# Four attention layers on one core: maxima from three leading products, and where the stacked keys lie

## The chip, the core and the metric

One core of one Trainium2 chip runs the whole program. The metric is the device time of one execution in microseconds (us). An instruction of TensorE is said to be on PE, of VectorE on DVE, of ScalarE on ACT, of GpSimd on POOL; SP is SyncE, which only issues DMAs and waits. A number like L1826 is a line of the kernel before.

## The reference

2,048 tokens of width 256 go through four layers. Each is cross attention to 1,601 context rows of width 192, with a residual, then a feed-forward part with experts, with a residual. Cut to what matters:

```python
q = (layernorm(x) @ Wq + bq) / sqrt(dh)      # 16 heads of 16 in layers 0, 1, 3; 8 heads of 32 in layer 2
k, v = ctx @ Wk + bk, ctx @ Wv + bv          # 1601 keys
x = x + softmax(q @ k.T) @ v @ Wo + bo       # per head, 2048 x 1601 scores
x = x + experts(layernorm(x))                # differs from layer to layer
```

All is float32.

## The kernel before

**Split products.** A score in float32 is built from bf16 parts. Query and key are each split into three bf16 parts (0 is the leading one), and six of the nine products of parts are kept. For a head of 16, the six lie on top of one another in the contraction of one matmul: `KS` (k_stack) holds key parts 0, 1, 2, 0, 1, 0 on partitions 0 to 95, `QS` (q_stack) holds query parts 0, 0, 0, 1, 1, 2. Partition 96 is the mask or zero, 97 to 99 are ones, against which `QS` carries the negative row maximum in three bf16 parts. In layer 2 (heads of 32) the six take two matmuls (`sub` 0 and 1), the first with the leading three.

**The attention loop.** Tokens are taken 512 at a time (`it`, four of them), heads in four groups `g` (four heads a group, two in layer 2), keys in 13 blocks `k` of 128. I call one `k` a slot: 16 groups of 13, so 208 slots in a layer. In a slot PE computes the scores (`scores`, L1863, 128 keys by 512 queries, bf16, four matmuls in every layer), ACT takes the exponential (L986), and PE multiplies the probabilities of the slot before with the values (`weigh`, L1877, float32). Each `weigh` matmul is 32 columns of stationary wide (64 in layer 2) and writes a 32- or 64-partition part of one PSUM bank, so four (two) of them lie side by side in the array.

**Side jobs.** The row maximum must be known before the scores of its group. It is found one to two groups ahead: a `max` job (L1826) computes 128 queries by 400 or 401 keys into one of three PSUM banks in turn, and DVE reduces it (L1257). A group needs 64 such jobs (32 in layer 2), dealt out as five a slot (two or three in layer 2), besides a few jobs that turn, scale and project (`turn`, `den`, `spread`, `out`, and in the first iteration `turn_x` and `query`). A job waits until DVE is done with the job three before it. The first 88 (44) max jobs of a layer run ahead of the loop (`side_prologue`); I call that the prologue. In the loop two jobs go ahead of the first score matmul and the others are spread behind each of the four score pieces.

**Loads.** All loads of keys, queries and feed-forward weights are issued by SP in program order, on one hardware queue. `next_keys` runs at the start of the feed-forward part of layers 0 to 2: it stores the eight pieces of split keys as POOL finishes them, and in layers 0 and 2, after the fourth and the eighth, waits for them to land and issues 12 loads into `KS` (L461). `load_queries` issues six loads and one of ones (L474 to L480), `store_max_rows` one load of the maxima (L494).

Of the kernel before, what the change touches and what calls it, by code (L numbers as in the profile page):

```python
# [6 lines left out]
P = 128  # L7
NT = T // P
Q = 512
# [26 lines left out]

class Count:
# [27 lines left out]

def side_schedule(g, hpg, first, last):
# [11 lines left out]
    late = [("max", (g + 1) % NG, u, c) for u in range(half, units) for c in range(4)] if nxt1 else []  # L78
    early = [("max", (g + 2) % NG, u, c) for u in range(half) for c in range(4)] if nxt2 else []
# [19 lines left out]
def max_jobs(g, hpg, lo, hi):  # L99
    return [("max", g, u, c) for u in range(lo, hi) for c in range(4)]  # L100
# [35 lines left out]
def build(nc, A, out):  # L136
# [13 lines left out]
    with ctx:  # L150
# [46 lines left out]
        with att:  # L197
# [5 lines left out]
            KS = sb("k_stack", [100, 16, S], bf16, att)  # L203
            V = sb("v", [P, NK, 512], f32, att)
            QS = [sb(f"q_stack{i}", [100, 4, Q], bf16, att) for i in range(4)]
# [9 lines left out]
        with ln2:  # L215
            sb("skip_sums", [P, 4 * 2 * Q + 2 * Q + 16 + Q + NG * Q], f32, ln2)
            sb("skip_keys", [100, 16, S], bf16, ln2)
            sb("skip_values", [P, NK, 512], f32, ln2)
            XN = sb("xn", [P, NT, D], f32, ln2)
# [100 lines left out]
        s_ks = [sem(f"s_ks{g}") for g in range(NG)]  # L320
        s_ql = [sem(f"s_ql{i}") for i in range(4)]
# [59 lines left out]


        @block.sync
        def _(sp):
# [34 lines left out]
            def load_constant_rows(L):  # L419

                ones_flat = const_rows[0:1, 0:S]
                rows = [(96, mask_row if L == 3 else zero_row)]
                if L in (0, 2):
                    rows += [(97, ones_flat), (98, ones_flat), (99, ones_flat)]
                for row, src in rows:
                    sp.dma_start(KS[row:row + 1, :, :], src.unsqueeze(1).to_broadcast([1, 16, S]))\
                      .then_inc(s_ksc, 16)
# [26 lines left out]
            def load_keys(L, g):  # L454

                dh, nsub, hpg = ATT[L]["dh"], ATT[L]["nsub"], ATT[L]["hpg"]
                for row in range(6):
                    part = [0, 1, 2, 0, 1, 0][row]
                    src = k_parts[part].rearrange("(h d) s -> d h s", d=dh)[:, g * hpg:(g + 1) * hpg, :]
                    r, sub = (row, 0) if nsub == 1 else (row % 3, row // 3)  # L460
                    sp.dma_start(KS[r * dh:(r + 1) * dh, 4 * g + sub:4 * g + 4:nsub, :], src)\  # L461
                      .then_inc(s_ks[g], 16)

            def load_queries(L, t, buf):
# [5 lines left out]
                dst = QS[buf]  # L470
                if a["nsub"] == 1:
                    for row, part in enumerate([0, 0, 0, 1, 1, 2]):
                        src = q_parts[part].rearrange("(h d) t -> d h t", d=dh)[:, g * hpg:(g + 1) * hpg, cols]
                        sp.dma_start(dst[row * dh:(row + 1) * dh, :, :], src).then_inc(s_ql[buf], 16)  # L474
                else:
                    for row, part in enumerate([0, 0, 0, 1, 1, 2]):
                        src = q_parts[part].rearrange("(h d) t -> d h t", d=dh)[:, g * hpg:(g + 1) * hpg, cols]
                        r = row % 3
                        sp.dma_start(dst[r * dh:(r + 1) * dh, row // 3::2, :], src).then_inc(s_ql[buf], 16)
                sp.dma_start(dst[96:97, :, :], ones_row).then_inc(s_ql[buf], 16)  # L480

            def store_max_rows(L, g):
# [11 lines left out]
                sp.dma_start(QS[g][96:100, 0:4:a["nsub"], :], src).then_inc(s_mr, 16)  # L494
# [25 lines left out]
            load_keys(0, 0)  # L520
            load_keys(0, 1)

            for L in range(4):
# [8 lines left out]
                if L == 0:  # L532
# [3 lines left out]
                    load_keys(0, 2)  # L536
                    load_keys(0, 3)
# [1727 lines left out]
```

## Time and profile before

| | |
|---|---|
| Time, median of 3 runs | 4478.63 us (4469.84 to 4485.76) |
| Profiled execution: its own time, its span | 4481.04 us, 4479.3 us |
| Granted clock of PE, mean over the span | 0.926 |
| PE busy | 4004.6 us (89%) |
| DVE busy | 2650.2 us (59%) |
| ACT busy | 1937.9 us (43%) |
| POOL busy | 322.4 us (7%) |

The granted clock is a share of 2.4 GHz. A busy PE is one with a matmul in flight; successive matmuls overlap, so the distance between two starts is what one costs, not its duration.

### The profile page before, as it was taken

The numbers are of one execution on the slowest core, as the hardware profiler recorded it, in microseconds if no ns is written. First come the engines' busy times: TensorE is split into PE (matmuls) and PEld (weight loads), VectorE is DVE, ScalarE is ACT, GpSimd is POOL, SyncE is SP. The second block draws the span as 40 slices with busy tenths as digits, with TensorE's granted clock in tenths as the row PEclk, the third lists the DMA queues.
The fourth block names the chain that finished last, engine by engine and source line by source line (L and its number), as shares of the span: only waits on it lengthen the run. The fifth ranks groups of instructions, "written<-read, shape, count | busy, mean of one in ns | idle before, by whom it ended". The sixth has DMA issues, their size and how long they took to land. (4 is left out here: it accounts for less than half of the span.)

```text
span 4479.3 us, 60914 instructions
## 1 busy us (share of the span) xinstructions
PE 4004.6 (89%) x19174; PEld 1813.1 (40%) x19175; DVE 2650.2 (59%) x5801; ACT 1937.9 (43%) x2306; POOL 322.4 (7%) x588
## 2 busy tenths in 40 slices
PE   5999999799899999948993999998889999996894
PEld 2333333566333333335662343443532333333563
DVE  5888785445788888532224555443258887874122
ACT  1567667222166766712331334333103666763110
POOL 2100000200010000040002100000101000000202
PEclk8999999799699999958996999999697999997997
DMA  6000000400000000052104000000400000001145
GB/s 126 25 16 13 13 9 2 82 19 19 24 26 16 10 13 9 1 198 95 32 29 104 26 15 12 12 8 19 66 20 27 20 11 13 10 4 67 61 143 106
DMA packets 131861, 170.58 MB, mean 38 GB/s; under 512 B 30840, under 2 KB 111936, under 8 KB 129539
## 3 DMA queue, kind: packets, MB, share of 16 engines
q1 hardware_dynamic: 121986, 136.07, 11.7%
q0 software_dynamic: 9600, 31.04, 2.4%
q8 instruction: 149, 2.44, 0.2%
q14 instruction: 126, 1.02, 0.1%
HBM read 114.12 MB, written 54.66 MB: 38 GB/s over the span
## 5 line engine op out<-in xcount | busy, mean ns | idle before, releaser
L1257 DVE TENSOR_REDUCE mx<-ps 128x1 f32<-128x400 f32 (+1 forms) x3584 | 1809.0, 565 | 491.1 <-PE ps L1826 482.5
L986 ACT ACTIVATE probs<-ps,zero_col 128x1024 f32<-128x1024 f32 (+1 forms) x1040 | 1113.3, 1111 | 889.5 <-PE ps L1863 889.4
L1826 PE MATMUL ps<-k_stack,q_stack 97*128 97x400 bf16 (+3 forms) x4096 | 1219.5, 347 | 74.5 <-issue 34.8
L1863 PE MATMUL ps<-q_stack,k_stack 100*128 100x512 bf16 (+2 forms) x3328 | 1081.6, 382 | 4.0 <-ACT probs L986 4.0
L1877 PE MATMUL ps<-probs,v 128*32 128x512 f32 (+2 forms) x5824 | 891.9, 607 | 0.2 <-ACT probs L986 0.2
L1826 PEld LDWEIGHTS ps<-k_stack,q_stack 97*128 97x128 bf16 (+1 forms) x4096 | 343.9, 98 | 1173.7 <-DVE mx L1257 712.3
L986 ACT ACTIVATE probs<-ps,mask_col 128x1024 f32<-128x1024 f32 (+1 forms) x416 | 441.0, 1110 | 259.6 <-PE ps L1863 259.6
L1863 PEld LDWEIGHTS ps<-q_stack,k_stack 100*128 100x128 bf16 (+2 forms) x3328 | 324.7, 100 | 315.7 <-ACT probs L986 55.8
L1532 DVE SCALAR_TENSOR_TENSOR x_res<-ps,comb,x_res 128x256 f32<-128x256 f32 x336 | 148.3, 482 | 175.7 <-PE ps L2027 168.6
L1877 PEld LDWEIGHTS ps<-probs,v 128*32 128x32 f32 (+2 forms) x5824 | 140.0, 111 | 228.4 <-issue 220.2
L2027 PE MATMUL ps<-w_down_s,h_t_s 128*128 128x256 f32 x640 | 149.5, 381 | 4.3 <-ACT h_t_s L1088 4.1
L2091 PE MATMUL ps<-w_all,xn_t 128*128 x624 | 144.6, 385 | 3.8 <-ACT xn_t L1056 2.4
L2012 PE MATMUL ps<-xn_t,w_up_s 128*128 128x512 f32 x320 | 147.2, 592 | 0.8 <-issue 0.8
L2070 PE MATMUL ps<-w_all,xn_t 128*128 x312 | 142.7, 600 | 0.4 <-issue 0.4
L2027 PEld LDWEIGHTS ps<-w_down_s,h_t_s 128*128 128x128 f32 x640 | 120.6, 190 | 50.7 <-issue 35.5
L1848 PE MATMUL ps<-wo,o_t 128*128 128x256 f32 x512 | 130.7, 405 | 11.0 <-DVE mx L1257 7.6
L2091 PEld LDWEIGHTS ps<-w_all,xn_t 128*128 128x128 f32 x624 | 118.1, 192 | 43.0 <-issue 28.4
L1056 ACT ACTIVATE xn_t<-ps,tile_bias 128x128 f32<-128x128 f32 x312 | 84.7, 383 | 99.6 <-PE ps L2082 99.4
L1088 ACT ACTIVATE h_t_s<-ps 128x512 f32<-128x512 f32 x80 | 46.7, 596 | 177.0 <-PE ps L2012 176.9
L740 POOL MEMSET wv<- 1x256 f32 x4 | 1.2, 304 | 1670.6 <-DVEq L376 1670.3
L1848 PEld LDWEIGHTS ps<-wo,o_t 128*128 128x128 f32 x512 | 99.3, 200 | 40.7 <-DVE mx L1257 20.5
L2045 PE MATMUL ps<-w_up_s,xn_t 128*128 128x512 f32 x256 | 112.2, 601 | 0.8 <-DVE x_res L1499 0.8
(250 smaller groups left out, 2823.9 us busy)
## 6 DMA issues: line engine op xcount, KB each, us to landing
q_stack<-q_parts SPq DMA_DIRECT2D x384, 64.0 KB, 2.2
k_stack<-k_parts SPq DMA_DIRECT2D x96, 200.1 KB
q_parts<-qk_part SPq DMA_DIRECT2D x32, 384.0 KB, 2.5
w_up<-in_up SPq DMA_DIRECT2D x17, 704.0 KB, 4.3
x_place<-zeros POOLq DMA_DIRECT2D x2, 5120.0 KB, 28.6
k_parts<-qk_part SPq DMA_DIRECT2D x24, 384.0 KB, 3.2
w_all<-in_up SPq DMA_DIRECT2D x5, 1024.0 KB, 21.4
w_all<-in_down SPq DMA_DIRECT2D x5, 1024.0 KB, 23.6
```

Source lines behind the costliest of these rows:

```text
L986: act.activation(PR[pair[0] % 4][0:r, :, :], PS[0:r, 2 * b:2 * b + 2, :], ACT.Exp, bias=mask_col[0:r, k:k + 1] if L == 3 else zero_col[0:r ...
L1257: ins = dve.reduce_max(MX4[g % 2][:, u, c:c + 1], PS[:, bank, 0:CK[c]], AX.X)
L1532: dve.scalar_tensor_tensor(X[:, t, :], PS[:, b, 0:D], c, X[:, t, :], ALU.mult, ALU.add).then_inc(s_yf, 1)
L1826: last = mm(PS[:, bank, 0:CK[c]], QS[g][0:rows, s, qt * P:(qt + 1) * P], KS[0:rows, ks0, CKO[c]:CKO[c] + CK[c]], start=sub == 0, stop=sub ...
L1848: last = mm(PS[:, bank, 0:D], OT[:, g, i * P:(i + 1) * P], WO[:, g, :], start=g == 0, stop=g == NG - 1)
L1863: last = mm(PS[0:r, b + i, :], KS[0:rows, (g * hpg + jj) * nsub + sub, k * P:k * P + r], QS[g][0:rows, slot_of(jj) + sub, :], start=sub == ...
L1877: last = mm(PS[pw * jj:pw * jj + pw, 4, :], V[0:r, k, (g * hpg + jj) * pw:(g * hpg + jj) * pw + pw], PR[used[0] % 4][0:r, i, :], start=k = ...
L2012: last = mm(PS[0:rows, b, :], up[:, k, off + at:off + at + rows], xnT[:, k, c * Q:(c + 1) * Q], start=k == 0, stop=k == 1)
L2027: last = mm(PS[:, b, 0:D], HTF[(c - 1) % 2][0:rows, t, i * P:(i + 1) * P], WDF[par][0:rows, t, :], start=t == 0, stop=t == len(ft) - 1)
L2045: last = mm(PS[:, t % 8, :], xnT[:, k, t * P:(t + 1) * P], WUS[par][:, k * 512:(k + 1) * 512], start=k == 0, stop=k == 1)
L2070: last = mm(PS[:, half, :], XT1[par][:, k * P:(k + 1) * P], w1.rearrange("p a f -> p (a f)"), start=k == 0, stop=k == 1)
L2091: last = mm(PS[:, 4 + par, 0:D], HB[:, q * P:(q + 1) * P], w2.rearrange("p a f -> p (a f)"), start=q == 0, stop=q == NF // P - 1)
```

## The change

1. **Layout, layers 0, 1, 3.** Even heads of a group keep partitions 0 to 99, in another order: the three leading products (key 0 by query 0, key 1 by query 0, key 0 by query 1) on 0 to 47, the mask and the ones on 48 to 51, the other three on 52 to 99. Odd heads have the leading three on 64 to 111, mask and ones on 112 to 115, and four more products on 0 to 63.
2. **Max jobs.** In layers 0, 1, 3 a max job contracts over 49 partitions (0 to 48 or 64 to 112) in place of 97. In layer 2 it is one matmul (the first `sub`, 97 partitions) in place of two. In layers 0, 1, 3 jobs of an even and an odd head alternate.
3. **Order in a slot.** Two jobs (one in layer 2) ahead of the scores, up to two behind the last score, the rest between.
4. **Loads.** A group's keys take 13 loads in place of 6 in layers 0, 1, 3, its queries 15 in place of 7, its maxima 2 in place of 1, its constant rows 8 in place of 4 (layer 3: 8 in place of 1; layer 1: none, in place of 1). The keys of layers 1 and 3 are loaded by POOL, after the eighth split and once all pieces have landed; SP goes on without them.

```diff
+ROWS = ([(0, 0, 0), (16, 1, 0), (32, 0, 1), (52, 2, 0), (68, 1, 1), (84, 0, 2)],
+        [(64, 0, 0), (80, 1, 0), (96, 0, 1), (0, 2, 0), (16, 1, 1), (32, 0, 2), (48, 2, 1)])
+MROW, MAX_ROWS, ALL_ROWS = (48, 112), ((0, 49), (64, 113)), (100, 116)
...
+def max_order(hpg):
+    if hpg == 2:
+        return [(u, c) for u in range(2 * TPQ) for c in range(4)]
+    return [((2 * j + odd) * TPQ + t, c) for j in range(2) for t in range(TPQ) for c in range(4) for odd in range(2)]
...
+def places(n, npair):
+    if npair == 1:
+        return [min(n, 1), max(n - 1, 0) // 2, max(n - 1, 0) - max(n - 1, 0) // 2]
+    ahead, end = min(n, 2), min(max(n - 2, 0), 2)
+    rest = n - ahead - end
+    mid = (rest + 2) // 3
+    return [ahead, (rest - mid + 1) // 2, mid, (rest - mid) // 2, end]
...
                     for u in range(8):
                         store_key_parts(u)
-                        if L != 1 and u % 4 == 3:
-                            wait_landed(kd)
-                            load_keys(L + 1, u // 2 - 1)
-                            load_keys(L + 1, u // 2)
...
+                if L in (0, 2):
+                    for c in staged.landed["key"]:
+                        pool.wait_ge(c.sem, c.at())
+                    for g in range(NG):
+                        load_keys(pool, L + 1, g)
...
-                        for sub in range(nsub):
-                            rows = 97 if sub == 0 else 96
-                            s = slot_of(j) + sub
-                            ks0 = (g * hpg + j) * nsub + sub
-                            last = mm(PS[:, bank, 0:CK[c]], QS[g][0:rows, s, qt * P:(qt + 1) * P],
-                                      KS[0:rows, ks0, CKO[c]:CKO[c] + CK[c]], start=sub == 0, stop=sub == nsub - 1)
+                        lo, hi = MAX_ROWS[j % 2] if nsub == 1 else (0, 97)
+                        last = mm(PS[:, bank, 0:CK[c]], QS[g][lo:hi, slot_of(j), qt * P:(qt + 1) * P],
+                                  KS[lo:hi, (g * hpg + j) * nsub, CKO[c]:CKO[c] + CK[c]], start=True, stop=True)
...
-                            for job in slot[:2]:
-                                side(job)
-                            cut = [2 + n for n in chunk_of(max(len(slot) - 2, 0), 2 * npair)]
+                            jobs = list(slot)
+                            share = places(len(slot), npair)
                             for j in range(npair):
                                 for i in range(2):
+                                    for _ in range(share[2 * j + i]):
+                                        side(jobs.pop(0))
                                     scores(g, k, j, i)
-                                    for job in slot[cut[2 * j + i]:cut[2 * j + i + 1]]:
-                                        side(job)
+                            for job in jobs:
+                                side(job)
```

## Rows read from the trace of the kernel before

**Rows 1.** The page: the costliest DVE group; stores of key pieces, with KB and us to landing.
```profile
L1257 DVE TENSOR_REDUCE mx<-ps 128x1 f32<-128x400 f32 (+1 forms) x3584 | 1809.0, 565 | 491.1 <-PE ps L1826 482.5
...
k_parts<-qk_part SPq DMA_DIRECT2D x24, 384.0 KB, 3.2
```
**Rows 2.** Windows: stretch, length, PE, PEld, DVE, ACT, POOL busy, clock, DMA share, GB/s.
```profile
336.00:448.00 112.00, 111.72 (x674) 39.07 (x666) 97.78 (x207) 82.38 (x82) 0.00 (x0) 1.00 0.05 13
...
2688.00:2800.00 112.00, 110.99 (x528) 42.34 (x526) 56.83 (x117) 44.84 (x43) 0.00 (x0) 1.00 0.04 12
```
**Rows 3.** Timeline of layer 0, an ordinary slot: start, length, engine, line, shape, count, idle before.
```profile
412.68 0.33 PE L1826 MATMUL ps<-k_stack,q_stack 97*128 97x401 bf16 x1
...
412.85 0.38 PE L1863 MATMUL ps<-q_stack,k_stack 100*128 100x512 bf16 x1
...
413.07 0.33 PE L1826 MATMUL ps<-k_stack,q_stack 97*128 97x400 bf16 x1
...
413.46 0.33 PE L1826 MATMUL ps<-k_stack,q_stack 97*128 97x400 bf16 x1
...
413.72 1.07 PE L1877 MATMUL ps<-probs,v 128*32 128x512 f32 x8
...
414.72 0.51 PE L1826 MATMUL ps<-k_stack,q_stack 97*128 97x400 bf16 x2
...
415.10 2.50 DVE L1257 TENSOR_REDUCE mx<-ps 128x1 f32<-128x400 f32 x5 [0.33 <-PE ps L1826]
...
416.55 1.06 PE L1877 MATMUL ps<-probs,v 128*32 128x512 f32 x8
```
**Rows 4.** Timeline of PE in layer 2, a slot with three max jobs.
```profile
2680.05 1.08 PE L1877 MATMUL ps<-probs,v 128*64 128x512 f32 x4
...
2681.06 0.86 PE L1826 MATMUL ps<-k_stack,q_stack 97*128 97x400 bf16 x4
...
2683.07 1.08 PE L1877 MATMUL ps<-probs,v 128*64 128x512 f32 x4
```
**Rows 5.** Layer 3, feed-forward: weight loads of the turning matmuls, then a PE row.
```profile
4231.22 0.14 PEld L2153 LDWEIGHTS ps<-ident,x_expert 128*128 128x128 f32 x1
4231.53 0.40 PEld L2153 LDWEIGHTS ps<-ident,x_expert 64*128 64x128 f32 x3 [0.17 <-issue]
4232.10 0.14 PEld L2153 LDWEIGHTS ps<-ident,x_expert 64*128 64x128 f32 x1 [0.17 <-issue]
...
4236.73 6.73 PE L2172 MATMUL ps<-x_expert_t,w_up 128*128 128x320 f32 x24
```
**Rows 6.** Timelines of SP, POOL, ACT, PE and DVE at the start of layer 0's feed-forward part.
```profile
835.86 7.03 SPq L461 DMA_DIRECT2D k_stack<-k_parts  x12
842.94 22.41 SPq L437 DMA_DIRECT2D k_parts<-qk_part  x4
...
838.16 1.15 POOL L749 TENSOR_TENSOR qk_part<-qk,qk_part 128x512 bf16<-128x512 f32 x1
...
859.78 0.60 ACT L922 ACTIVATE qk<-ps 128x512 f32<-128x512 f32 x1 [22.23 <-DMA k_parts<-qk_part]
...
861.20 1.22 PE L1736 MATMUL ps<-wv,ctx_a 128*128 128x256 f32 x2 [20.96 <-ACT v L933]
...
848.04 0.42 DVE L1431 TENSOR_TENSOR comb<-prob_s,r_s 128x256 f32<-128x256 f32 x1
```
**Rows 7.** Timeline of PE, the same place in layer 2.
```profile
3197.57 1.22 PE L1736 MATMUL ps<-wv,ctx_a 128*128 128x256 f32 x2 [14.65 <-ACT v L933]
```
**Rows 8.** Timeline of SP and PE before the first max job of layer 1.
```profile
1172.42 2.69 SPq L474 DMA_DIRECT2D q_stack<-q_parts  x6
1175.16 0.53 SPq L480 DMA_DIRECT2D q_stack<-const_rows  x1
...
1177.29 8.03 PE L1826 MATMUL ps<-k_stack,q_stack 97*128 97x401 bf16 x17 [8.33 <-issue]
```
**Rows 9.** Timeline of POOL, a load that it issues in layer 1.
```profile
2027.62 0.58 POOL L854 DMA_DIRECT2D w_all<-in_down  x1
```

More of the change, by code:

```diff
@@ L77, in side_schedule @@
     half = units * 3 // 8
-    late = [("max", (g + 1) % NG, u, c) for u in range(half, units) for c in range(4)] if nxt1 else []
-    early = [("max", (g + 2) % NG, u, c) for u in range(half) for c in range(4)] if nxt2 else []
+    late = max_jobs((g + 1) % NG, hpg, half, units) if nxt1 else []
+    early = max_jobs((g + 2) % NG, hpg, 0, half) if nxt2 else []
     jobs = late + early[:6] + ([("turn", (g + 1) % NG)] if nxt1 else []) + early[6:]
@@ L320, in build @@
         s_ks = [sem(f"s_ks{g}") for g in range(NG)]
+        s_kt = [sem(f"s_kt{g}") for g in range(NG)]
         s_ql = [sem(f"s_ql{i}") for i in range(4)]
@@ L380, in key_rows, with load_keys @@
             return P if k < NK - 1 else KREM
+        def load_keys(eng, L, g):
+            dh, nsub, hpg = ATT[L]["dh"], ATT[L]["nsub"], ATT[L]["hpg"]
+            done = s_kt[g] if L in (1, 3) else s_ks[g]
+            heads = k_parts.rearrange("r (h d) s -> r d h s", d=dh)[:, :, g * hpg:(g + 1) * hpg, :]
+            if nsub == 1:
+                for odd in range(2):
+                    for row, part, _ in ROWS[odd]:
+                        eng.dma_start(KS[row:row + dh, 4 * g + odd:4 * g + 4:2, :], heads[part][:, odd::2, :])\
+                           .then_inc(done, 16)
+            else:
+                for i, (_, part, _) in enumerate(ROWS[0]):
+                    sub, r = i // 3, i % 3 * dh
+                    eng.dma_start(KS[r:r + dh, 4 * g + sub:4 * g + 4:2, :], heads[part]).then_inc(done, 16)
         @block.sync
@@ L421, in load_constant_rows @@
                 ones_flat = const_rows[0:1, 0:S]
[L422 to L427, printed above, removed]
+                rows = [mask_row if L == 3 else zero_row] + [ones_flat] * 3
+                for i, src in enumerate(rows):
+                    if ATT[L]["nsub"] == 1:
+                        for odd in range(2):
+                            sp.dma_start(KS[MROW[odd] + i:MROW[odd] + i + 1, odd::2, :],
+                                         src.unsqueeze(1).to_broadcast([1, 8, S])).then_inc(s_ksc, 16)
+                    else:
+                        sp.dma_start(KS[96 + i:97 + i, 0::2, :], src.unsqueeze(1).to_broadcast([1, 8, S]))\
+                          .then_inc(s_ksc, 16)
             def store_key_parts(u):
```

83 lines of the change are left out of this document (44 added, 39 removed).

## The prediction

> **What bounds the kernel now.** I read the page first: DVE's largest group, the reductions of the maxima, spends its idle time almost wholly (482.5 of 491.1 us) waiting for PE's max matmul [rows 1]. So DVE waits for PE, not the reverse. The windows say the same of whole stretches of the loop: in 112 us PE is busy 111.7 and DVE 97.8 in layer 0, and 111.0 against 56.8 in layer 2, both with the clock at 1.00, 2.4 GHz [rows 2]. Then the timeline of one slot, where the costs are distances between starts. In layer 0 a max matmul is followed by the next start after 0.17 us (412.68 to 412.85), a score matmul after 0.22 (412.85 to 413.07), a weigh block with what follows it takes 1.00 (413.72 to 414.72), and a slot repeats every 2.83 us (413.72 to 416.55) [rows 3]. Check: 5 x 0.17 + 4 x 0.22 + 1.00 = 2.73, and 0.10 more lies ahead of weigh. DVE does five reductions in 2.50 us and idles 0.33: it could carry a slot of about 2.5 and no less. In layer 2 a slot of three jobs (six max matmuls) takes 3.02 us, with DVE half idle [rows 2, 4].
>
> **What a change of array shape costs.** Score and max matmuls use all 128 rows and columns of the array; weigh uses strips of 32 columns. The last max of the slot starts at 413.46, streams 0.17, and weigh starts not at 413.63 but at 413.72: 0.09 to 0.10 us lost. Weigh is two rounds of 512 float32 columns; at the 0.87 ns a column that float32 costs (6.73 us for 24 matmuls of 320) that is 0.89, so 0.10 of its 1.00 is lost on leaving [rows 3, 5]. The same loss appears where only the number of rows changes. In layer 3's turning, two matmuls of 128 rows and columns (2 x 0.107 us at this rate, less its rounding) stand before one of 64 rows, but its weight load starts 0.31 us after the first's: 0.10 lost. From there to the next 64-row one is 0.57, of which 0.27 is streaming: 0.30 for two more changes and the loads that they expose. And each 64-row load stands behind 0.17 us of idle loader, marked as issue: it was not drawn ahead [rows 5]. I take 0.096 for the change itself and 0.013 for the bf16 load that can no longer be hidden (the two max matmuls after a weigh take 0.51 to the end of the second, 0.01 more than 0.17 + 0.33), together 0.109 us. A contraction of 49 rows at partition 0 or 64 is such a 64-row shape, so every run of max jobs in layers 0, 1, 3 is now fenced by two changes.
>
> **Layers 0, 1, 3, the loop.** I counted with the schedule's own functions, all 208 slots of a layer. The loop holds 936 max jobs. Before, PE changes shape 415 times (in and out of weigh). After, an ordinary slot reads: 2 max, 2 scores, 1 max, 2 scores, 2 max, weigh, so six changes in place of two; over the layer 1,313, that is 898 more. 898 x 0.109 = 97.9 us more. Against it, 320 runs hold two max jobs, one on each row half. They write different banks, and I expect them to run side by side as the strips of weigh do, which start within a few ns (eight in 1.07 us, where one after the other would need eight times 0.43) [rows 3]. With 0.007 between the two starts a pair saves 0.165: 320 x 0.165 = 52.8 us less. Halving the rows by itself saves nothing, since 97 or 100 rows, 400 or 512 columns, all cost what their columns do at 2.4 GHz, 0.17 and 0.22 [rows 3]. Net +45 a layer, +135 in all. Part of it falls in slots where DVE holds PE up today (the one after `turn`, those with a normalized chunk, those with `out`), and there added PE time is free. I take 8 us of the 98 a layer, an estimate with nothing and 25 as its ends, so +110. Bounds: pair starts 0.007 to 0.172 apart (the latter is no overlap, +158), change 0 to 0.15 us (the second is half of 0.30).
>
> DVE does not become the bound in an ordinary slot: 2.93 us leave it 0.4 idle. The three banks hold: of the last two jobs before weigh, DVE ends the second about 0.1 us after weigh, when the next pair's banks have been free for 0.5. ACT has 2 x 1.06 in a slot.
>
> The Trainium skill, TensorE: Matmul & The Clock Gate, Part 3 (packing small matmuls), says tiles on different row groups run at once, about 4 ns apart, and measured 3.07 times for four such tiles. No row here shows row halves; by the 3.07 each further tile would cost a tenth of a matmul, and my sum would be some 10 us higher.
>
> **Layer 2.** One max matmul in place of two: 468 jobs in the loop x 0.172 (0.167 of streaming and 0.005 to the next start) = 80.5 us less. 97 rows is no 64-row shape, so no change of shape is added. DVE (1.5 us of 3.02) and ACT (1.06) leave room for a slot of 2.50 [rows 2, 4]. The max rows are asked for later in the slot (`turn` now stands at its end), but they need some 5.5 us of the 6 left in the group; no stall. -80.
>
> **Feed-forward, layers 0 and 2.** SP issues 12 key loads (7.03 us) and then the store of the fifth key piece; that store waits behind 2.4 MB, ACT resumes at 859.78 after 22.23 us idle, PE at 861.20 after 20.96 [rows 6]. POOL had the piece ready at 839.3 [rows 6], and a store lands in 3.2 us [rows 1]; so ACT would resume at 842.5, 17.3 us sooner. What is late next: DVE's routing ends at 848.5 [rows 6], while PE would have the rest of its values from 844 to about 851, so nothing takes it back. In layer 2 it is 14.65 us of PE's idle time [rows 7]. With 2 us, an estimate, for a clock that the shorter pause leaves up, -34 in all. The moved loads: 52 on POOL; at 0.58 us each [rows 9] 30 us, at most 2 each, so done well before layer 1 (its first max job comes 316 us after the stall ends) and within layer 2's feed-forward part. Expert weights are asked for one expert ahead and have many us to land beside them.
>
> **Starts of layers 0, 1, 3.** The first max job waits for the loads of queries: seven issues in 3.3 us, 0.47 each; it starts 0.05 after the last of them is through [rows 8]. Eight more issues are 3.7 us, three times 11, and layer 0's queries stand behind 8% more key bytes, 2 us: +13. In the loop SP has 15 issues (7 us) in 37; hidden. Layer 2's prologue now keeps PE less busy and I expect the low clock to reach a few us into its loop, and two issues of maxima in place of one: +4.
>
> **Sum.** 110 - 80 - 34 + 13 + 4 = +13. The profiled execution took 4481.0; the median of the runs is 2.4 lower. 4478.6 + 13 + 2 (rounding toward the profiled one) = 4494.
>
> **Rivals.** (a) *The change of height is cheap, and it ends faster.* Only six turning matmuls a tile show a change of rows, in float32; bf16 streams may need less. Each 10 ns less on 2,694 changes is 27 us, so it decides from 0.10 downward: at 0.05 the time is about 4335, at nothing 4230. For it: bf16 weight loads are short. Against: column strips after bf16 max matmuls cost the same 0.10 [rows 3]. 27%. (b) *The pairs don't overlap, or only partly, or the half loads are exposed.* The float32 loads above cost 0.05 each where 0.30 was lost to two changes; if a half-height bf16 load costs that in place of 0.013, 1,848 runs add 0.04, +74: 4568; no overlap at all +158: 4652. The 0.172 apart can also come from the second waiting for its bank, but the banks are free. 20%. (c) *The moved loads collide*: the store stays late or weights come late, the 34 are not earned: 4528. 5%. (d) *The clock falls in the loop* because a slot has 0.66 us of pauses; were a tenth of the three loops granted the lower level (1.2 GHz), where PE's work takes twice as long, it would be some +200: 4690. Nothing in the windows shows such a fall while PE works [rows 2]. 3%. (e) DVE's stalls absorb more than 8 us a layer, or the layer 2 slots gain from the order: 4450, 5%.
>
> **Chances and range.** My forecast holds 40%, with its own range 4465 to 4530, from 0.09 to 0.12 for a change and 0.007 to 0.03 for a pair. What this measurement can tell from no change is 0.3%, 13.4 us, so 4465 to 4492 is no change: of the 40%, 8 are faster, 16 the same, 16 slower. With (a) and (e) faster 40%, with (b), (c), (d) slower 44%. The range reaches to a change of 0.06 below (4370) and to pairs two thirds serial above (4610).
>
> **What would show it.** In the timeline of a layer 0 slot: two max matmuls starting within 10 ns, then 0.27 us to the score; slot 2.93. A slot of 2.5 would be rival (a), of 3.1 to 3.3 rival (b). The attention loops of layers 0, 1, 3 some 35 us longer each, that of layer 2 80 shorter; no 21 us gap at L1736; the first max job of layer 1 starts 3.7 us later after its queries' store. The prediction is wrong if the change of height is not 0.1 us.

## The result, and the profile after

| | before | after |
|---|---|---|
| Time, median of 10 runs each on one chip | 4471.7 us (4466.0 to 4485.8) | 4491.65 us (4479.6 to 4503.9) |
| Ratio, 95% interval | | 1.004 [1.0026, 1.0055] |
| Span of the profiled execution | 4479.3 us | 4482.8 us |
| Granted clock, mean over the span | 0.926 | 0.914 |
| PE busy, DVE busy | 4004.6, 2650.2 us | 4050.0, 2714.5 us |

The kernel became 0.4% slower: 18 us by the ratio, 20 by the medians. The spans differ by only 3.5 us. This execution of before lost about 14 us at its very end (410.8 us from layer 3's last `weigh` to the end of the span, 397.0 after), in a feed-forward part that the change doesn't touch. Profiled executions of other kernels below have the long end or the short one with the same code there (409.0 in l2one, 395.9 in ahead3), so I leave the end out of the comparison.

The page of after names the same bound as [rows 1], DVE waiting for PE's max matmul, and one thing that it did not have, a wait for weights:

```profile
L1298 DVE TENSOR_REDUCE mx<-ps 128x1 f32<-128x400 f32 (+1 forms) x3584 | 1870.2, 568 | 465.6 <-PE ps L1868 415.1
...
L2055 PE MATMUL ps<-xn_t,w_up_s 128*128 128x512 f32 x320 | 149.7, 601 | 6.3 <-DMA w_down_s<-in_down 5.5
```

By stage, in us, from the first start of a max or score matmul and the end of the last `weigh` matmul:

| | before | after | difference |
|---|---|---|---|
| Up to the first max job | 64.6 | 67.8 | +3.2 |
| Prologue of layer 0 (first max job to first score) | 51.6 | 76.6 | +25.0 |
| Loops of layers 0, 1, 3 (first score to last `weigh`) | 661.6, 664.0, 665.8 | 691.6, 693.8, 694.8 | +88.7 |
| Prologue and loop of layer 2 | 26.8, 633.4 | 24.5, 556.4 | -79.3 |
| Prologues of layers 1 and 3 | 46.0, 46.0 | 45.9, 45.9 | -0.2 |
| Last `weigh` of layer 0 to first max job of layer 1 | 399.4 | 395.0 | -4.4 |
| the same, layer 1 to 2 | 558.9 | 554.0 | -4.9 |
| the same, layer 2 to 3 | 250.2 | 239.6 | -10.6 |

The sum is +17.5, what the timed runs say.

Windows of after (columns as in [rows 2]): the prologue of layer 0 with 3.8 us ahead of it, the four loops, and one group of 13 slots, from one `weigh` to the thirteenth behind it, at full clock:

```profile
64.00:144.00 80.00, 69.36 (x159) 25.35 (x159) 45.62 (x95) 10.08 (x23) 9.61 (x12) 0.50 0.35 73
144.40:836.00 691.60, 684.34 (x3771) 193.08 (x3769) 538.61 (x1103) 456.74 (x446) 21.21 (x24) 0.98 0.05 13
1276.90:1970.60 693.70, 686.22 (x3771) 193.11 (x3769) 538.73 (x1103) 456.95 (x446) 21.20 (x24) 0.98 0.05 13
2549.10:3105.50 556.40, 553.51 (x2471) 204.26 (x2469) 320.37 (x635) 248.34 (x238) 21.22 (x24) 0.99 0.05 14
3391.00:4085.80 694.80, 687.09 (x3771) 193.63 (x3769) 538.76 (x1103) 456.89 (x446) 21.21 (x24) 0.98 0.05 13
...
562.38:602.82 40.44, 40.44 (x236) 10.67 (x234) 35.34 (x73) 28.66 (x29) 0.00 (x0) 1.00 0.05 13
```

The same three kinds of window of before:

```profile
64.60:116.20 51.60, 44.76 (x159) 20.25 (x160) 45.99 (x97) 10.06 (x23) 9.56 (x12) 0.86 0.55 102
...
116.20:777.90 661.70, 649.45 (x3770) 229.58 (x3768) 521.49 (x1102) 455.86 (x446) 21.18 (x24) 1.00 0.04 13
...
508.91:547.90 38.99, 38.85 (x235) 13.63 (x234) 34.17 (x74) 28.54 (x29) 0.00 (x0) 1.00 0.04 13
```

Two things are to be seen. This group takes 1.45 us more, with the same matmuls to do and PE never idle. The 16 groups of a loop are not alike: where both kernels run at full clock, the difference is from 0.03 us (the last, which has no max jobs) to 2.05, and I estimate some 20 us for the sixteen, of the loop's 30. And the clock differs: 0.50 through the whole prologue of layer 0 where it was 0.86, and 0.98 in the loops. The clock's own record says where: after layer 0's first score it stays at the lower level for another 11.2 us (3.7 before) and falls three times more for 3.4, 3.4 and 6.8 us (not once in the same loop of before); in layer 3 one fall lasts 17.1 us. That is some 20 us more a loop at half speed, so some 10 us lost, the other third of the 30.

An ordinary slot of layer 0 after, beside [rows 3]:

```profile
391.24 1.07 PE L1919 MATMUL ps<-probs,v 128*32 128x512 f32 x8
392.24 0.34 PE L1868 MATMUL ps<-k_stack,q_stack 49*128 49x400 bf16 x2
...
392.52 0.61 PE L1905 MATMUL ps<-q_stack,k_stack 100*128 100x512 bf16 x2
392.62 2.69 DVE L1298 TENSOR_REDUCE mx<-ps 128x1 f32<-128x400 f32 x5 [0.21 <-PE ps L1868]
393.06 0.34 PE L1868 MATMUL ps<-k_stack,q_stack 49*128 49x400 bf16 x1
...
393.33 0.61 PE L1905 MATMUL ps<-q_stack,k_stack 100*128 100x512 bf16 x2
393.87 0.34 PE L1868 MATMUL ps<-k_stack,q_stack 49*128 49x400 bf16 x2
394.14 1.06 PE L1919 MATMUL ps<-probs,v 128*32 128x512 f32 x8
```

The slot is 2.90 us (391.24 to 394.14), before 2.83. Two max matmuls in 0.34 us have started together: a pair and the step to the score cost 0.28 (392.24 to 392.52), a single max and the step 0.27 (393.06 to 393.33). Of each, 0.17 is streaming and 0.10 the change of shape. Two scores and the step back to max take 0.54 (392.52 to 393.06), of which 0.43 is streaming (2 x 512 columns at 2.4 GHz). Over such steps in the loops of layers 0, 1, 3 at full clock, the start of the next matmul is 99 to 111 ns later than streaming alone (steps between the same two kinds in before: mostly 2 to 7 ns), and the two of a pair start 3 to 4 ns apart. The Trainium skill, TensorEngine Tiling (Array Packing), Key Properties, says that changing the tiling mode drains TensorE, without a figure; the trace shows a loss at each change, as the page would have it, of about 0.10 us.

### The profile page after: what moved, and what is told of

Its sections match the earlier page's. It is cut to its first block and busy times, and to the rows that moved or that the text cites. A ratio compares the mean times of both kernels' runs of the same rounds, so it can differ in the third digit from the quotient of the medians.

```text
span 4482.8 us, 60654 instructions
## 1 busy us (share of the span) xinstructions
PE 4050.0 (90%) x18662; PEld 1659.1 (37%) x18663; DVE 2714.5 (61%) x5801; ACT 1942.9 (43%) x2306; POOL 374.9 (8%) x692
## 5 line engine op out<-in xcount | busy, mean ns | idle before, releaser
L1298 DVE TENSOR_REDUCE mx<-ps 128x1 f32<-128x400 f32 (+1 forms) x3584 | 1870.2, 568 | 465.6 <-PE ps L1868 415.1
L1905 PE MATMUL ps<-q_stack,k_stack 100*128 100x512 bf16 (+4 forms) x3328 | 1028.1, 389 | 4.0 <-ACT probs L1027 4.0
L1868 PE MATMUL ps<-k_stack,q_stack 49*128 49x400 bf16 (+3 forms) x3584 | 947.2, 359 | 79.3 <-issue 42.3
L1919 PE MATMUL ps<-probs,v 128*32 128x512 f32 (+2 forms) x5824 | 904.0, 616 | 0.2 <-ACT probs L1027 0.2
L1868 PEld LDWEIGHTS ps<-k_stack,q_stack 49*128 49x128 bf16 (+1 forms) x3584 | 253.2, 94 | 1368.0 <-DVE mx L1298 827.0
L1905 PEld LDWEIGHTS ps<-q_stack,k_stack 100*128 100x128 bf16 (+4 forms) x3328 | 246.3, 99 | 364.2 <-issue 190.3
L1623 DVE COPY xn_t<-ps 128x512 f32<-128x512 f32 x78 | 53.9, 692 | 93.6 <-PE ps L2113 93.6
```

The source lines that it names most:

```text
L1298: ins = dve.reduce_max(MX4[g % 2][:, u, c:c + 1], PS[:, bank, 0:CK[c]], AX.X)
L1868: last = mm(PS[:, bank, 0:CK[c]], QS[g][lo:hi, slot_of(j), qt * P:(qt + 1) * P], KS[lo:hi, (g * hpg + j) * nsub, CKO[c]:CKO[c] + CK[c]], s ...
L1905: last = mm(PS[0:r, b + i, :], KS[0:rows, (g * hpg + jj) * nsub + sub, k * P:k * P + r], QS[g][0:rows, slot_of(jj) + sub, :], start=sub == ...
L1919: last = mm(PS[pw * jj:pw * jj + pw, 4, :], V[0:r, k, (g * hpg + jj) * pw:(g * hpg + jj) * pw + pw], PR[used[0] % 4][0:r, i, :], start=k = ...
```

## The experiments

Eleven kernels, in three groups by the question they answer. Each ran in turn with the kernel before on its chip; the stages of all stand in one table behind them.

### What do the half-height max jobs cost in the loop?

**nopair**: the changed kernel, but max jobs of one head follow one another, so that no two neighbours lie on different row halves.

```diff
-    if hpg == 2:
-        return [(u, c) for u in range(2 * TPQ) for c in range(4)]
-    return [((2 * j + odd) * TPQ + t, c) for j in range(2) for t in range(TPQ) for c in range(4) for odd in range(2)]
+    return [(u, c) for u in range(hpg * TPQ) for c in range(4)]
```

> The changed kernel with its max jobs in the order of heads again, so that two neighbouring ones are of the same head and lie on the same row half. Theory (pairs on opposite halves run side by side, 3 ns apart in the changed kernel's trace): two of one half come 167 ns and more apart, so 320 pairs in each of three loops lose 0.164 us each, 157 us in all; time about 4650, ratio to the kernel before 1.039, an ordinary slot of layers 0, 1, 3 at 3.33 us in place of 3.00. Rival (the two starts lie close together but the pair saves little, since a third stage holds the slot, say DVE or the banks): below 4540. The shape changes stay at about 0.10 us each in both.

Measured: 4698.22 us, ratio 1.0489 [1.0456, 1.0521]. The group at full clock:

```profile
602.47:646.31 43.84, 43.84 (x235) 10.98 (x234) 35.57 (x73) 28.64 (x29) 0.00 (x0) 1.00 0.04 12
```

3.40 us more than after. In after's trace 22 pairs of this group start within 4 ns, in nopair's one, so a pair is worth 3.40 / 21 = 0.162 us, nearly the 0.167 that a max matmul streams: the pairs overlap fully. Other groups hold fewer pairs (the last none), and over a loop I estimate some 45 us, of 59 to 70. The rest is a clock that falls for long stretches here (44, 44, 38 and 20 us), its mean 0.900: 31 to 54 us more of a loop than in after are at the lower level, with as many changes of shape. That also makes the 0.01 by which the ratio passes what was expected.

**three**: the changed kernel, with the side jobs of a slot grouped so that PE changes shape four times, not six.

```diff
-    ahead, end = min(n, 2), min(max(n - 2, 0), 2)
-    rest = n - ahead - end
-    mid = (rest + 2) // 3
-    return [ahead, (rest - mid + 1) // 2, mid, (rest - mid) // 2, end]
+    ahead, end = min(n, 3), min(max(n - 3, 0), 2)
+    return [ahead, 0, n - ahead - end, 0, end]
```

> The changed kernel with the jobs of a slot placed three ahead, none between, up to two behind (anything over five between the second and third score). An ordinary slot of layers 0, 1, 3 then has four changes of shape in place of six. Theory (PE's sum sets the slot, a change costs 0.10 to 0.11 with the load it exposes): two changes less are 0.22 us less, from 3.00 to 2.78, some 150 such slots a layer and half of that in the rest: 100 to 120 us less than the changed kernel, about 4375, ratio 0.978; loops of layers 0, 1, 3 near 655. Rival (DVE or the three banks take over when jobs come three at a time): slots at 2.9 to 3.0, PE waiting for DVE at the third job, time 4440 to 4490.

Measured: 4424.59 us, ratio 0.9866 [0.9847, 0.9885]. A slot in the timeline, then the window of a group:

```profile
600.32 1.06 PE L1917 MATMUL ps<-probs,v 128*32 128x512 f32 x8
601.32 0.51 PE L1866 MATMUL ps<-k_stack,q_stack 49*128 49x400 bf16 x3
601.77 1.04 PE L1903 MATMUL ps<-q_stack,k_stack 100*128 100x512 bf16 x4
602.74 0.41 PE L1866 MATMUL ps<-k_stack,q_stack 49*128 49x400 bf16 x2
603.08 1.06 PE L1917 MATMUL ps<-probs,v 128*32 128x512 f32 x8
```
```profile
561.44:600.32 38.88, 38.74 (x235) 11.73 (x234) 34.31 (x73) 28.53 (x29) 0.00 (x0) 1.00 0.05 14
```

The slot was foreseen (2.76), the total was not. The two jobs at its end now wait for a bank instead of overlapping (0.34 us from the first to `weigh`, 602.74 to 603.08, against 0.27 for a pair), slots with other side jobs still change shape more often than before's, and a group of 13 comes to 38.88 us, only 0.11 less than before's 38.99, with 59 changes of shape in the trace where before has 28 and after 85. The loops took 667 to 672, with stretches of low clock in them of up to 10.2 us. So with four changes of shape in an ordinary slot, half height wins nothing against full height.

**tallall**: the changed kernel, with full-height max jobs in layers 0, 1, 3 (on the odd heads' stack, so the maxima of even heads are left out).

```diff
-                        lo, hi = MAX_ROWS[j % 2] if nsub == 1 else (0, 97)
+                        lo, hi = (0, 113) if nsub == 1 else (0, 97)
+                        if nsub == 1:
+                            j |= 1
```

> The changed kernel with one thing changed: in layers 0, 1 and 3 every max job, in the prologue and in the loop, contracts over 113 partitions of an odd head (0 to 112) in place of the 49 of its own head; the maxima are those of odd heads only, with seven products. Layout, loads, queues, order in a slot and layer 2 are those of the changed kernel. Max and score matmuls then have one array shape and nothing overlaps in pairs. Theory (the changes of shape, less the pairs, are what the loops of layers 0, 1 and 3 lost): each loop takes 661 to 667 us in place of 692 to 695, an ordinary slot 2.83 us, the granted clock stays up in the loop, the prologue of layer 0 takes 52 to 57 us, and the kernel comes to 4365 to 4385 us beside a kernel before of 4475, ratio 0.976 to 0.980. Rival (the loops lost to the order in a slot, to the finer loads or to the dips of the clock that these bring): loops of 680 to 695 us, ratio 0.985 to 1.000.

Measured: 4367.95 us, ratio 0.976 [0.9745, 0.9775]. Windows of its three loops, and a group:

```profile
121.50:782.80 661.30, 648.43 (x3770) 234.06 (x3768) 522.22 (x1102) 455.31 (x446) 21.23 (x24) 1.00 0.05 14
1222.30:1885.70 663.40, 650.80 (x3770) 235.07 (x3768) 522.63 (x1102) 455.53 (x446) 21.23 (x24) 0.99 0.05 13
3305.80:3968.10 662.30, 648.58 (x3770) 234.24 (x3768) 522.20 (x1102) 455.34 (x447) 21.23 (x24) 1.00 0.05 13
...
508.14:547.12 38.98, 38.83 (x234) 13.89 (x233) 34.17 (x73) 28.54 (x29) 0.00 (x0) 1.00 0.05 13
```

The loops are those of before, and so is the clock (one fall, of 3.4 us in layer 1). Layout, 13 loads a group, and the order in a slot cost nothing. All of the loops' 93 us against this kernel, and the clock's further falls, come with the half-height max matmuls, their changes of shape and pairs included. The rival is out.

**ahead3**: the order of three without half height: the kernel before, with one max matmul in layer 2, POOL's key loads, and in layers 0, 1, 3

```diff
-                            for job in slot[:2]:
+                            ahead = min(len(slot), 3) if npair == 2 else 2
+                            for job in slot[:ahead]:
                                 side(job)
-                            cut = [2 + n for n in chunk_of(max(len(slot) - 2, 0), 2 * npair)]
+                            if npair == 2:
+                                rest = len(slot) - ahead
+                                cut = [ahead, ahead, ahead + max(rest - 2, 0), ahead + max(rest - 2, 0), len(slot)]
+                            else:
+                                cut = [2 + n for n in chunk_of(max(len(slot) - 2, 0), 2 * npair)]
```

> The kernel before (full-height stack, one array shape in all max and score matmuls) with the single max matmul in layer 2, the key loads on POOL's queue (24 a layer) and, in layers 0, 1 and 3, another order in a slot: three jobs ahead of the scores, none between, up to two behind the last score, the rest before it. No half-height matmuls and no pairs. It asks what the order is worth where no change of array shape is paid. Theory: with three jobs waiting for DVE ahead of the scores and two behind them, the slot is set by what PE streams (four scores, five max jobs, one group of weighing, about 2.72 us) in place of 2.83, so a loop of 208 slots gives 20 us and the three together some 55 to 60 us beyond the 2.4% of the two other edits: 4315 to 4330 us, ratio 0.964. Rival (order does nothing here, since DVE's own 2.50 us and its waits set the slot): 4380 us, 0.976, slot 2.83. Rival (the dense order holds the clock no better than before, or the two late jobs delay the weighing): above 0.976.

Measured: 4373.97 us, ratio 0.9792 [0.9772, 0.9812]; loops 663.4, 663.9 and 669.2 us. A slot:

```profile
416.45 1.06 PE L1878 MATMUL ps<-probs,v 128*32 128x512 f32 x8
417.45 0.69 PE L1827 MATMUL ps<-k_stack,q_stack 97*128 97x400 bf16 x3
...
417.98 1.03 PE L1864 MATMUL ps<-q_stack,k_stack 100*128 100x512 bf16 x4
...
418.84 0.51 PE L1827 MATMUL ps<-k_stack,q_stack 97*128 97x400 bf16 x2
419.28 1.07 PE L1878 MATMUL ps<-probs,v 128*32 128x512 f32 x8
```

My theory missed. The slot is 2.83 us as before, because PE already had no idle time in it: 1.00 + 0.53 + 0.86 + 0.44. I had put the sum of PE's work at 2.72 and left out the change of shape ahead of `weigh`, 0.10 us, which the prediction had read. With one array shape, order alone buys nothing.

### Why did the prologue of layer 0 lose 25 us?

**halfpro**: the kernel before, with half-height max jobs in that prologue alone (the parts stacked in the order that is given for l2one below).

```diff
                             rows = 97 if sub == 0 else 96
+                            if half_height[0]:
+                                rows = 48
...
+                half_height[0] = L == 0
                 behind = projection_order(0, 1) if L == 0 else []
```

> The kernel before with one thing changed in the prologue of layer 0: there alone, the max jobs contract over the first 48 partitions in place of 97 (the maxima of those 88 jobs come from three products; everything behind the prologue is as before; key parts are stacked in the order 0, 1, 0, 2, 1, 0 and query parts 0, 0, 1, 0, 1, 2). The number of instructions, their columns and their order stay. Theory (half the height keeps the granted clock down): the clock stays at 0.50 through the whole prologue, which takes 72 to 77 us from the first max job to the first score in place of 51.6, and the kernel is 0.5% slower (4507 us against 4487, ratio 1.005). Rival (the changed kernel's 76.6 us come from its finer loads or from the alternation of even and odd heads): the prologue stays at 51 to 55 us and the ratio at 1.000.

Measured: 4491.44 us, ratio 1.0058 [1.0035, 1.008].

**tallpro**: the reverse, the changed kernel with full height there alone.

```diff
                         lo, hi = MAX_ROWS[j % 2] if nsub == 1 else (0, 97)
+                        if tall[0]:
+                            j, lo, hi = j | 1, 0, 113
...
+                tall[0] = L == 0
                 behind = projection_order(0, 1) if L == 0 else []
```

> The changed kernel with one thing changed in the prologue of layer 0: there alone each max job contracts over 113 partitions of an odd head (0 to 112) in place of the 49 of its own head, so that the 88 maxima of the prologue are those of odd heads only, with seven products. Loads, order and everything behind the prologue are those of the changed kernel. Theory (height keeps the clock down): the clock rises to 1.00 within the prologue, which takes 52 to 57 us in place of 76.6, and the kernel is some 22 us faster than the changed one (ratio to the kernel before 0.999 in place of 1.004). Rival (loads, order): the prologue stays at 74 to 77 us and the ratio at 1.004.

Measured: 4465.44 us, ratio 0.9995 [0.9983, 1.0008]. The prologue's window in halfpro:

```profile
64.20:141.30 77.10, 75.91 (x160) 27.99 (x161) 46.22 (x97) 10.06 (x23) 9.60 (x12) 0.50 0.37 68
```

and in tallpro:

```profile
70.00:121.60 51.60, 44.62 (x160) 20.04 (x158) 45.83 (x97) 9.97 (x23) 9.59 (x12) 0.86 0.54 102
```

Both kernels do what the theory said and neither what the rival said. The same matmuls, by number, columns and order, take 76.6 and 77.1 us at half height (after, halfpro) and 51.6 and 51.9 at full (before, tallpro), on either layout. At half height the profile shows PE busy for 75.91 of 77.10 us and the clock nevertheless never leaves 1.2 GHz, from 55.6 us to 3 us into the loop; at full height it rises to 2.4 GHz 4 to 5 us after the first max job (at 68.7 us in before, at 74.8 in tallpro) and stays up for 37.5 us. In the other full-height prologues of layer 0 it rises within 21 us; in none of the half-height ones does it rise. The first 4.1 us of before, at whose end its clock rises, and of halfpro, where it doesn't, then the prologue of layer 1 in before:

```profile
64.60:68.70 4.10, 4.00 (x7) 1.57 (x8) 2.02 (x4) 0.00 (x0) 0.00 (x0) 0.50 0.53 178
```
```profile
64.20:68.30 4.10, 3.99 (x7) 1.53 (x8) 2.02 (x4) 0.00 (x0) 0.00 (x0) 0.50 0.54 177
```
```profile
1177.30:1223.30 46.00, 42.64 (x91) 9.51 (x92) 44.66 (x97) 0.00 (x0) 0.00 (x0) 0.50 0.11 34
```

The Trainium skill, TensorE: Matmul & The Clock Gate, Part 1, says that the gate follows how busy PE has been. By the busy share alone halfpro should have risen as before did (3.99 us busy beside 4.00); the measurement decides, and here the height of the max jobs counted too. Height alone does not lift the clock: in layers 1 and 3 the max jobs stand without projections between them, DVE is busy nearly throughout, and the clock stays at 0.50 in the full-height prologue of before as in the half-height one of after (46.0 and 45.9 us).

One thing no run separates. Half height also brings changes of shape between max jobs and projections, 36 in halfpro's prologue where before has 2. At 0.11 to 0.14 us each, as their steps in halfpro show, they are some 4 of the 25 us; whether it is the rows or these changes that keep the clock down is not shown. In the loops the number of changes is not all: nopair has after's number and is longer at the lower level.

### What is the other half of the change worth?

**l2one**: the kernel before, with one max matmul in layer 2 (and the parts of keys and queries stacked so that the first `sub` holds the leading three products, as in the changed kernel: key parts 0, 1, 0, 2, 1, 0 by query parts 0, 0, 1, 0, 1, 2).

```diff
-                        for sub in range(nsub):
-                            rows = 97 if sub == 0 else 96
...
+                        last = mm(PS[:, bank, 0:CK[c]], QS[g][0:97, slot_of(j), qt * P:(qt + 1) * P],
+                                  KS[0:97, (g * hpg + j) * nsub, CKO[c]:CKO[c] + CK[c]], start=True, stop=True)
```

> The kernel before with one part of the change alone: one max matmul in place of two in layer 2 (its maxima come from the three leading products; the parts are stacked so that these three are the first). Theory: 468 jobs in the loop save 0.165 to 0.172 us each, loop of layer 2 from 633 to 556 us as in the changed kernel, prologue 2 us shorter: -79 us, about 4393, ratio 0.982. Rival (the order inside a slot, not the missing matmul, gave part of the 77 us): a loop of layer 2 of 580 or more, ratio 0.987 or above.

Measured: 4397.41 us, ratio 0.9803 [0.9786, 0.9821]; layer 2's loop 554.2 us, its prologue 24.8. The missing matmul makes all of it; the rival is out.

**poolkeys**: the kernel before, with the keys of layers 1 and 3 loaded by POOL. **l2pool**: both edits.

```diff
                     for u in range(8):
                         store_key_parts(u)
-                        if L != 1 and u % 4 == 3:
-                            wait_landed(kd)
-                            load_keys(L + 1, u // 2 - 1)
-                            load_keys(L + 1, u // 2)
...
+                if L in (0, 2):
+                    for c in staged.landed["key"]:
+                        pool.wait_ge(c.sem, c.at())
+                    for g in range(NG):
+                        load_keys(pool, L + 1, g)
```

> The kernel before with the move of the key loads alone: the keys of layers 1 and 3 are loaded from POOL's queue once all pieces have landed, in 24 loads a layer as before, not 52. Layout, max jobs and order as before. Theory: the two waits in front of the first expert go (21.0 us in layer 0, 14.7 us in layer 2), less a later wait for weights of an expert that lie behind the 24 key loads (some 5 to 9 us in layer 0), so 22 to 28 us less: ratio 0.994 to 0.995, 4460 us against 4487. Rival (the moved loads are free for the experts): 34 us less, 0.992. Rival (nothing gained, since POOL's loads delay the experts by as much): 1.000.

> The kernel before with the two parts of the change that cost nothing by my account: one max matmul in layer 2, and the keys of layers 1 and 3 loaded from GpSimd's queue, 24 loads a layer in the old layout in place of 52. Layers 0, 1, 3 keep the full-height max jobs, the old layout and the old order. Theory: -79 for layer 2, -17 and -15 for the two feed-forward parts, less what late expert weights cost (5.5 us in the changed kernel with 52 loads): 4365 to 4375, ratio 0.977. Rival (the moved loads give nothing once expert weights come late behind them): as with layer 2 alone, 4390 or more.

Measured: poolkeys 4452.79 us, ratio 0.9965 [0.9954, 0.9977]; l2pool 4382.18 us, 0.9759 [0.9733, 0.9785]. For poolkeys that is 16 us, below every figure that I gave except the last rival's. In layer 2 the part between the loops is 14.6 us shorter. In layer 0 it is only 4.8 shorter, and the timeline of poolkeys shows why (SP's and POOL's queues, then PE):

```profile
857.77 12.37 POOL L392 DMA_DIRECT2D k_stack<-k_parts  x24 [3.38 <-DMA k_parts<-qk_part]
...
874.22 0.37 SPq L595 DMA_DIRECT2D w_up_s<-in_up  x1
874.69 0.47 SPq L597 DMA_DIRECT2D w_down_s<-in_down  x1
...
898.42 5.19 PE L2017 MATMUL ps<-xn_t,w_up_s 128*128 128x512 f32 x8 [10.61 <-DMA w_down_s<-in_down]
```

An expert takes some 14 us (13.8 between the issues of two pairs of weights), and its weights are asked for one expert ahead. The pair issued at 874.22 and 874.69 lands at 891.5 and 898.3 us, 17.3 and 23.6 us later, behind 24 loads of 200 KB that POOL put out in 12 us; in spread, below, a pair lands 2 us after its issue. The changed kernel has the same wait, shorter by half (5.46 us). Its timeline, then its DMA view from 905 to 950 us (KB each, us from issue to landing):

```profile
910.50 26.04 POOL L414 DMA_DIRECT2D k_stack<-k_parts  x52 [3.24 <-DMA k_parts<-qk_part]
...
927.10 0.37 SPq L633 DMA_DIRECT2D w_up_s<-in_up  x1
...
927.57 0.46 SPq L635 DMA_DIRECT2D w_down_s<-in_down  x1
...
946.14 1.22 PE L2055 MATMUL ps<-xn_t,w_up_s 128*128 128x512 f32 x1 [5.46 <-DMA w_down_s<-in_down]
```
```profile
k_stack<-k_parts POOLq DMA_DIRECT2D x52, 100.1 KB, 9.8
...
w_up_s<-in_up SPq DMA_DIRECT2D x2, 128.0 KB, 13.4
w_down_s<-in_down SPq DMA_DIRECT2D x2, 128.0 KB, 15.3
```

**spread** (on l2pool) and **afterspread** (on the changed kernel): in layer 0, POOL holds a group's loads back until the next four experts are done.

```diff
                     for g in range(NG):
+                        if L == 0:
+                            pool.wait_ge(s_y, Y_FREE + (4 + 4 * g) * NT)
                         load_keys(pool, L + 1, g)
```

> The kernel before with the single max matmul in layer 2 and the key loads on POOL's queue, 24 a layer (4382 us, 0.976, with one wait of 8.9 us for an expert's weights in layer 0), and with one thing more: in layer 0, POOL holds back the six loads of group 0, 1, 2, 3 until experts 4, 8, 12, 16 have been computed. Theory (the weights came late because all 24 loads had been put in front of them at once): the wait of 8.9 us goes, nothing waits for weights longer than 1 us, and layer 0's feed-forward part, 393 us, shrinks by 7 to 9 us; ratio 0.974. Rival (a group of six loads delays one pair of weights as much as 24 do, so that four shorter waits come): nothing gained, 0.976.

> The changed kernel with the same hold in layer 0: POOL issues the 13 key loads of a group only when experts 4, 8, 12, 16 have been computed. Theory: the wait of 5.5 us for the third expert's weights goes; layer 0's feed-forward part 395 to 390 us; ratio to the kernel before 1.003 in place of 1.004. Rival (13 short loads at a time delay the weights anyway): 395 us, unchanged.

Measured: spread 4356.74 us, ratio 0.9734 [0.9721, 0.9747]; afterspread 4489.42 us, 1.0026 [1.0011, 1.0042]. In spread, POOL's first six loads and the group of the experts' matmuls read

```profile
913.16 3.32 POOL L392 DMA_DIRECT2D k_stack<-k_parts  x6 [62.87 <-PE ps L2030]
```
```profile
L2015 PE MATMUL ps<-xn_t,w_up_s 128*128 128x512 f32 x320 | 147.2, 592 | 0.8 <-issue 0.8
```

No wait for weights is left in either kernel. The part between the loops of layers 0 and 1 went from 393.4 to 383.4 us and from 395.0 to 387.3. Both theories held in the trace. In the timed runs the steps, 0.0025 and 0.0014 of the ratio, lie inside the intervals. spread is the best kernel of the study, 2.7% faster than before and 3.0% faster than the change; nothing in its layers 0, 1, 3 is half high.

### The stages of all kernels

In us, from each profiled execution. "0 to 1" is from the last `weigh` of layer 0 to the first max job of layer 1.

| | prologue 0 | loops 0, 1, 3 | loop 2 | 0 to 1 | 2 to 3 | ratio |
|---|---|---|---|---|---|---|
| before | 51.6 | 661.6, 664.0, 665.8 | 633.4 | 399.4 | 250.2 | 1 |
| after | 76.6 | 691.6, 693.8, 694.8 | 556.4 | 395.0 | 239.6 | 1.004 |
| nopair | 77.2 | 758.4, 753.0, 764.7 | 556.0 | 395.2 | 236.2 | 1.0489 |
| three | 76.9 | 667.4, 671.6, 669.5 | 556.2 | 395.0 | 237.0 | 0.9866 |
| tallall | 53.4 | 661.3, 663.4, 662.3 | 556.0 | 393.5 | 239.4 | 0.976 |
| ahead3 | 55.5 | 663.4, 663.9, 669.2 | 553.8 | 395.7 | 234.1 | 0.9792 |
| halfpro | 77.1 | 664.4, 666.5, 662.0 | 632.5 | 397.0 | 253.1 | 1.0058 |
| tallpro | 51.9 | 697.9, 699.0, 694.7 | 556.0 | 395.2 | 239.6 | 0.9995 |
| l2one | 54.8 | 666.8, 664.0, 661.9 | 554.2 | 395.9 | 249.0 | 0.9803 |
| poolkeys | 57.9 | 661.0, 661.8, 666.6 | 633.3 | 394.6 | 235.6 | 0.9965 |
| l2pool | 54.3 | 666.2, 666.7, 665.3 | 555.7 | 393.4 | 233.1 | 0.9759 |
| spread | 52.1 | 661.5, 667.0, 662.0 | 553.9 | 383.4 | 234.4 | 0.9734 |
| afterspread | 76.6 | 696.3, 701.5, 698.3 | 556.2 | 387.3 | 239.4 | 1.0026 |

Same code differs by up to 5 us in a loop and 6 in the full-height prologue, from where the clock steps.

## Why the prediction came out as it did

The time was right, 4494 against 4491.65, and so was the main mechanism. That the sum came so close is luck in part: the prologue of layer 0 (25 us) and the clock in the three loops (some 30) were priced at nothing, the feed-forward gain was put 11 too high, and against them the change of shape was priced too high and the waits that absorb it too low, together some 50 us. By its own steps:

- **The price of a change of shape: right, a tenth too much.** 0.096 us and 0.013 for the load were predicted, 0.109 together; the steps show 0.099 to 0.111 beyond streaming with the load in it, 0.097 more than an ordinary step, which has some 0.005 itself. Rivals (a) (cheap) and the second part of (b) (exposed loads) are out.
- **The pairs: right.** Predicted 0.165 us each with starts 0.007 apart; nopair gives 0.162, and the starts are 3 to 4 ns apart in 298 of the 320 pairs of a loop. The Trainium skill, TensorE: Matmul & The Clock Gate, Part 3, gives about 4 ns between tiles on different row groups; the trace agrees.
- **The loops of layers 0, 1, 3: right in kind, 20 us too much.** Predicted +37 each, measured +30.0, +29.8, +29.0. By my estimate some 20 of that are steady. The trace has 883 more changes; at 0.097 they are 86 us where the prediction had 98, and 298 pairs at 0.162 are 48 where it had 53. Of the 38 left, some 18 were absorbed where DVE held PE up before, where I took 8: rival (e) is true in that part. Steps of layer 0's loop that start over 0.03 us later than the median step of their kind fell from 167 to 32. The other 10 us a loop are the clock. The prediction read from two windows at 1.00 [rows 2] that it would not fall; the record of before has a fall of 3.4 us in layer 1's loop and one of 6.8 in layer 3's, and with half-height jobs there is more. The slot is 2.90 us, not 2.93.
- **Layer 2: right.** -80 predicted, -77.0 measured in the loop. The +4 for its prologue and the clock behind it did not come; the prologue became 2.3 shorter.
- **The feed-forward parts: a third too much.** Predicted -34. Without the later start of the next max job they are 8.4 (layer 0) and 14.5 (layer 2) shorter, 23 together. PE's wait of 20.96 us in layer 0 is gone. Layer 2's is exact (14.65 us of idle time). In layer 0 the failed step is "Expert weights are asked for one expert ahead and have many us to land beside them": they landed 14.6 and 18.5 us after their issue and PE stood still for 5.46. With the loads held back (afterspread) the same part is 15.7 shorter, near the 17.3 that were predicted. Rival (c), which I gave 5%, is true for a third of the term.
- **The starts of layers 0, 1, 3: right.** Predicted +13, measured 3.2 + 4.0 + 3.9 = 11. The profile of layer 1's start, beside [rows 8], shows the second seven loads and their row of ones in front of the max job:

```profile
1225.94 3.19 SPq L508 DMA_DIRECT2D q_stack<-q_parts  x7
1229.17 0.61 SPq L510 DMA_DIRECT2D q_stack<-const_rows  x1
...
1231.00 0.82 PE L1868 MATMUL ps<-k_stack,q_stack 49*128 49x401 bf16 x3 [12.31 <-issue]
```

- **The prologue of layer 0: missed, 25 us.** No step of the prediction costed it, since the matmuls there keep their number and columns. halfpro and tallpro show that the height of its max jobs decides it, mostly through the clock. Rival (d), 3%, said that the clock could fall in the loop "because a slot has 0.66 us of pauses". It did, for 25 to 31 us of each loop where (d) had a tenth of it, and it stayed down in the prologue, where pauses are not the cause: PE is busy 98% of halfpro's.

The sum with the measured terms: 88.7 (loops) - 79.3 (layer 2) - 22.9 (feed-forward) + 11.1 (starts) + 25.0 (prologue) - 4.9 (between layers 1 and 2) - 0.2 = +17.5. The 4.9 between layers 1 and 2 I did not foresee and did not follow up; kernels built on the changed one have 554.0 to 556.6 there, those built on the kernel before 556.7 to 559.9. It is left open.

Also open is why the falls of the clock in the loops come where they do, and whether the rows or the changes of shape bring them. That they come with the half-height max jobs is shown by tallall.

## What to carry to other kernels

Where PE is the bound, a matmul with half the rows costs what one with all of them does, and it wins only as the second of a pair; each run of such matmuls between full-height ones pays two changes of array shape, here 0.2 us against 0.16 won by a pair, so one pair between two changes loses. By these prices longer runs would win where PE is the bound, but that is not shown: three, with runs of three and two, came out even, and the prologues of layers 1 and 3, one run of 88, have DVE as their bound and took 45.9 us for 46.0. Look also at the clock in stretches of such matmuls just behind a slow start: there 88 half-height ones, with full-height projections between them, cost 25 us. A bulk load that is moved to a second queue is off the first queue, but not off the DMA engines: issue it in pieces behind the consumers of the small loads that it would delay.

## What the runs showed of the hardware

- A change between full-height and half-height matmuls costs 99 to 111 ns beyond streaming at 2.4 GHz; one between 128-column and 32-column shapes costs 96 to 98, in some steps up to 108.
- Half-height bf16 matmuls on the two row halves start 3 to 4 ns apart and a pair takes the time of one: 0.162 us saved of 0.167.
- With half-height max jobs in layer 0's prologue the granted clock stayed at 1.2 GHz over 77.1 us in which PE was busy for 75.9; at full height, with the same columns, it rose to 2.4 GHz 4 to 20 us behind the first of them. In the prologues of layers 1 and 3 it stayed at 1.2 GHz at either height, with PE busy for 42.6 of 46.0 us. In loops at 2.4 GHz with half-height jobs it fell for 3.4 to 27.3 us at a time, and up to 44 us with no pairs; at full height no fall in a loop was longer than 10.2 us.
- 24 or 52 loads, 4.9 or 5.3 MB, put out by POOL in 12 or 26 us made two pairs of 128 KB loads on SP's queue take 11 to 24 us to land, where they take 2 otherwise. PE waited 8.9 to 10.6 us behind the 24 larger ones, 5.0 to 5.5 behind the 52.
